# SyncE's order of the stacking and maxima transfers, and the place of 24 aggregations, in a patch-attention-feedforward kernel

## The chip, the cores and the metric

The kernel runs on one core of a Trainium2 chip. A core has five engines that run their own instruction streams side by side and wait for each other through semaphores: TensorE (PE), VectorE (DVE), ScalarE (ACT), GpSimd (POOL) and SyncE (SP), which here only issues transfers. The metric is the device time of one execution in microseconds (us), the median of several runs.

## The reference

Sixteen images of 3x64x64 are cut into patches at three scales along a Hilbert curve, embedded, interpolated to 256 tokens of width 192, and fused. Then follow a causal attention with 12 heads of width 16 and a fast feedforward layer, a walk down a binary tree of 21 nodes. Cut to what matters here:

```python
h = tok(x)                                            # (16, 256, 192), 16 images
qkv = (layernorm(h) @ W_attn + b_attn).reshape(16, 256, 3, 12, 16)
scores = einsum("bqhd,bkhd->bhqk", q, k) / 4          # causal mask: -inf above the diagonal
h = h + (softmax(scores) @ v).reshape(16, 256, 192) @ W_proj + b_proj
logits = layernorm(h) @ weights_in.T                  # (16, 256, 21)
# 10 steps: idx = 2 * idx + 1 + (logit[idx] > 0), gelu(logit) as coefficient of each node
h = h + coeff @ weights_out
```

Everything is float32 at the outside.

## The kernel before

**The work.** The images (`b`, 0 to 15) go through a pipeline of steps. In step b the scores of image b are computed for its row maxima, while the transposed scores of image b-1 go through the exponential, are cut to the causal triangle and weighted with the values, and while queries and keys of image b+2 are computed. The softmax needs the maximum of each row ahead of the exponential of the transposed scores, so scores are computed twice: once as rows (`scores`, L1437 and L1441) for VectorE's `row_max` (L933), and once transposed (`scores_t`, L1475 and L1479) for ScalarE's `exp` (L616). The negative maximum enters the transposed product as two more rows of the contraction.

**Parts.** Queries and keys are split into three bfloat16 parts (`PART`): ScalarE writes the first (`first_part`, L604, semaphore `p0_ok`, two calls per image, 3 activations), VectorE the remainder (`rest`, L946), ScalarE the second (`middle`, L610, `p1_ok`), GpSimd the third (`low`, L378, `p2_ok`). Six products of parts are stacked along the contraction: 6 blocks of 16 rows. `stack(f, w, n)` (L320) issues on SyncE the transfers that copy part n of the queries (w = 0, tile `QS` or `QSL`) or keys (w = 1, `KS` or `KSL`) of image f to their blocks: 3 transfers for part 0, 2 for part 1, 1 for part 2, so 12 per image, each 96 KB, from SBUF to SBUF. It waits first until the part is there for both calls. `maxima(b)` (L326) waits for `mt_ok` and issues the 12 KB transfer that puts the maxima of image b, as ScalarE leaves them in `MT` (L621), into rows 96 and 97 of image b's query stack. `scores_t(b, par, 0)` waits for it (`m_in`), `scores(b, par, 0)` for all stacks of image b (`stacked`).

**What sets the order.** Every engine's order is written by hand. SyncE runs its transfers strictly in the order of the code, and an unmet wait holds all behind it. In iteration n of its loop it issues the stacks of image n+1 and then the maxima of image n, so the stacks of image n+2 go behind the maxima of image n. In ScalarE's step b (f = b+2, d = b-1) stand: three exponentials of d, values of f, first part of f (one activation), four exponentials, first part of f (two activations), two exponentials, `middle(f, 0)`, `front`, `maxima(b)` (writes `MT`), `middle(f, 1)`. In TensorE's step b: `scores(b, 0)`, queries, `scores(b, 1)`, values, `scores_t(d, 0)`, `thirds`, and then `scores` and `scores_t` in turn. The stacks have a ring of four buffers, `PART` one of two.

**The first step.** `first_step` on each engine takes the row maxima of image 0 beside the rest of the token work. VectorE aggregates there the statistics of the 24 tiles of images 4 to 15 (`aggregate(OTHERS)`, L898), ScalarE takes the root (`deviations(3, OTHERS)`, L572), VectorE the reciprocal (`rstd(3, OTHERS)`, L906); the first user is the scaling of image 4 on ScalarE in step 1.

Of the kernel before, what the change touches and what calls it, by code (L numbers as in the profile page):

```python
# [5 lines left out]
B, CH, IMG = 16, 3, 64  # L6
# [23 lines left out]
SU = 9  # L30
# [35 lines left out]
def vit_tower_kernel(nc, x0, x1, x2, ix0, ix1, ix2, w0, w1t, w2t, wft, wfn, bcol, bf, bfc,  # L66
# [8 lines left out]
    with ctx:  # L75
# [3 lines left out]
        def sem(name):  # L79
            return ctx.enter_context(nc.semaphore(name))  # L80
# [113 lines left out]
        ht_ps, ht_ok = sem("ht_ps"), sem("ht_ok")  # L194
# [19 lines left out]
        st_ps, exp_ok, av_ps, ot_ok, cut_ok, carried = [sem(n) for n in ("st_ps", "exp_ok", "av_ps", "ot_ok", "cut_ok", "carried")]  # L214
# [29 lines left out]
        HEADS, SECOND, OTHERS = slice(0, 2 * TT), slice(2 * TT, 4 * TT), slice(4 * TT, NT)  # L244

        def parts(b):

            return PART[PARTS * (b.off % 2):PARTS * (b.off % 2 + 1)]
# [31 lines left out]
        def _(sp):  # L280
# [22 lines left out]
            def ones(i):  # L303

                sp.dma_start(KS[i][KQ:KM, :, :].rearrange("r h s -> r (h s)"), onesk).then_inc(ld_ones, 16)
# [9 lines left out]
            def stack(f, w, n):  # L315

                sp.wait_ge((p0_ok, p1_ok, p2_ok)[n], f.count(2, 2))
                dst = (QS, KS)[w][f.off % RING]
                for k in TERMS[w][n]:
                    sp.dma_start(dst[HS * k:HS * (k + 1), :, :].rearrange("r h s -> r (h s)"),  # L320
                                 parts(f)[n][EMB * w:EMB * (w + 1), :, :].rearrange("p m s -> p (m s)")).then_inc(stacked[w][f.off % 2], 16)

            def maxima(b):

                sp.wait_ge(mt_ok, b.count(1, 1))
                sp.dma_start(QS[b.off % RING][KQ:KM, :, :], MT[:, :]).then_inc(m_in, 16)  # L326

            first = Image(0, 0)
            for part in range(PARTS):
                for w in range(2):  # L330
                    stack(first, w, part)
            for n in range(B):
                b, f = Image(0, n), Image(0, n + 1)
                if n + 1 < B:
                    if n == 1:
                        sp.wait_ge(ht_ok, B)
                        ones(2)
                        ones(3)
                    if n > 2:
                        sp.wait_ge(st_ps, SU * (n - 2))  # L340
                    stack(f, 1, 0)
                    stack(f, 0, 2)
                    stack(f, 0, 1)
                    stack(f, 1, 2)
                    stack(f, 0, 0)
                    stack(f, 1, 1)
                maxima(b)

            for k in range(NQ - 1):
                sp.wait_ge(*added(k))  # L350
# [150 lines left out]
        def _(act):  # L501
# [68 lines left out]
            def deviations(round_, tiles):  # L570
                act.wait_ge(var_ok, round_)
                nc.scalar.activation(SD[:, tiles], VE[:, tiles], ACT.Sqrt).then_inc(sd_ok, 1)  # L572
# [45 lines left out]
            def maxima(b):  # L618

                act.wait_ge(mt_ps, b.count(1, 1))  # L620
                nc.scalar.mul(MT[:, :], BANK[O_BANK[1]][0:2 * H, 0:S // 2].bitcast(bf16), -1.0).then_inc(mt_ok, 1)  # L621
# [66 lines left out]
            first, second = Image(0, 0), Image(0, 1)  # L688

            def first_step():  # L690

                tokens(1, 5)
                front(Image(0, 2))
                tokens(1, 6)
                norm(Image(0, 3))
                tokens(1, 7)
                values(Image(0, 2))
                first_part(Image(0, 2), 0)
                first_part(Image(0, 2), 1)
                deviations(3, OTHERS)  # L700
                middle(Image(0, 2), 0)
                middle(Image(0, 2), 1)
                front(Image(0, 3))
                maxima(first)

            patches_t(0, 0)
            patches_t(0, 1)
# [110 lines left out]
        def _(dve):  # L818
# [76 lines left out]
            def aggregate(tiles):  # L895
                dve.wait_ge(stat, done[0])
                for k in range(tiles.start, tiles.stop):
                    nc.vector.bn_aggr(MV[:, k, :], ST[:, k, :]).then_inc(stat, 1)  # L898
                    done[0] += 1
                dve.wait_ge(stat, done[0])  # L900
                variances(tiles)

            def rstd(round_, tiles):

                dve.wait_ge(sd_ok, round_)
                nc.vector.reciprocal(RSTD[:, tiles], SD[:, tiles]).then_inc(rstd_ok, 1)  # L906
# [136 lines left out]
            first, second = Image(0, 0), Image(0, 1)  # L1043

            def first_step():

                row_max(first, 0, 0)
                row_max(first, 0, 1)
                row_max(first, 0, 2)
                statistics(1, 4)  # L1050
                row_max(first, 0, 3)
                statistics(1, 5)
                row_max(first, 0, 4)
                statistics(1, 6)
                row_max(first, 0, 5)
                statistics(1, 7)
                row_max(first, 0, 6)
                rest(Image(0, 2), 0)
                rest(Image(0, 2), 1)
                aggregate(OTHERS)  # L1060
                row_max(first, 0, 7)
                row_max(first, 0, 8)
                rstd(3, OTHERS)

            def first_low():
# [817 lines left out]
```

## Time and profile before

| | us |
|---|---|
| median of 3 runs | 324.56 |
| the three runs | 324.44, 324.56, 325.06 |
| the profiled execution | 324.9 |
| its span, first to last instruction | 323.2 |
| TensorE busy | 268.2 (83%) |
| VectorE busy | 240.4 (74%) |
| ScalarE busy | 202.4 (63%) |
| GpSimd busy | 196.5 (61%) |
| mean granted clock of TensorE | 0.966 of full |

Busy time is what an engine's instructions took; SyncE's issues of transfers are not counted as busy. The transfers of SyncE's queue take 33.7% of the 16 DMA engines' span. The span is that of the profiled execution, and all durations and places of the trace are from it, in us from its start. The time from issue to landing of a stacking transfer is 2.9 us at least, 3.6 in the median and 5.4 at most.

### The profile page before, as it was taken

How to read it: one execution, taken by the hardware profiler on the slowest of the kernel's cores; microseconds unless marked ns; L12 is line 12 of the kernel's file. 1: busy time of each engine (PE TensorE's matmuls, PEld its weight loads, DVE VectorE, ACT ScalarE, POOL GpSimd, SP SyncE). 2: the span in 40 equal slices, each digit the busy share in tenths (PEclk: the TensorE clock that was granted, in tenths of full speed). 3: DMA queues.
4: the chain of work that ended last, by engine and by line, in shares of the span. 5: the costliest groups of instructions: out<-in, count | busy, mean ns of one | idle time of the engine just before them, and what ended most of it. 6: DMA issues, size and time to landing. Idle time of an engine off the chain costs nothing.

```text
span 323.2 us, 7904 instructions
## 1 busy us (share of the span) xinstructions
PE 268.2 (83%) x2506; PEld 196.8 (61%) x2506; DVE 240.4 (74%) x1156; ACT 202.4 (63%) x429; POOL 196.5 (61%) x419
## 2 busy tenths in 40 slices
PE   0499887188787789999999999999989989999872
PEld 0465655077765466666666666667657578777662
DVE  2053887147496839999999999999989988876872
ACT  2653293047346918868778877876865854868770
POOL 3737777500204827778687778688668666556561
PEclk9999999679999959999999999999999999999997
DMA  5822332003970942444434534524432333000039
GB/s 126 235 54 39 85 69 44 16 2 77 130 89 31 125 119 30 114 84 102 125 85 101 129 87 99 127 90 100 110 102 88 110 103 52 2 4 3 0 107 285
DMA packets 27456, 28.13 MB, mean 87 GB/s; under 512 B 7186, under 2 KB 26704, under 8 KB 27416
## 3 DMA queue, kind: packets, MB, share of 16 engines
q1 hardware_dynamic: 23912, 24.56, 33.7%
q0 software_dynamic: 1568, 2.36, 3.2%
q10 hardware_dynamic: 1936, 0.72, 0.9%
q8 instruction: 20, 0.33, 0.5%
q14 instruction: 20, 0.16, 0.2%
HBM read 4.62 MB, written 3.15 MB: 24 GB/s over the span
## 4 chain that ended last, share of the span: by engine, by line
PE 41%; DVE 20%; POOL 14%; issue 9%; DMA 6%; SPq 5%; ACT 4%; POOLq 0%; ACTq 0%; DVEq 0%
POOL G L373 9%; DVE C L933 9%; PE bank L1497 6%; PE bank L1441 5%; SPq L320 4%; PE bank L1475 4%; PE bank L1412 3%; PE bank L1437 2%; PE bank L1500 2%; DMA G<-x,I 2%; POOL PT L400 2%; PE bank L1382 2%; PE bank L1530 2%; ACT PT L616 2%; PE bank L1479 2%
## 5 line engine op out<-in xcount | busy, mean ns | idle before, releaser
L933 DVE CUSTOM_DVE_ANT_0 C<-bank,MASKV 128x256 bf16<-128x256 f32 (+1 forms) x384 | 111.8, 352 | 18.8 <-PE bank L1441 11.2
L616 ACT ACTIVATE PT<-bank 128x512 f32<-128x512 f32 x144 | 81.8, 602 | 40.2 <-PE bank L1475 32.1
L400 POOL TENSOR_SCALAR_AFFINE_SELECT PT<-PT 128x256 f32<-128x256 f32 x144 | 66.4, 473 | 0.0
L396 POOL TENSOR_TENSOR CARRY<-CARRY 1x1 f32<-1x1 f32 x96 | 17.6, 183 | 46.7 <-ACT PT L616 46.7
L378 POOL TENSOR_TENSOR PART<-RES,PART 128x256 bf16<-128x256 f32 (+1 forms) x31 | 28.0, 904 | 21.1 <-ACT PART L610 21.1
L373 POOL DMA_INDIRECT G<-x,I x32 | 30.3, 947 | 14.2 <-issue 9.4
L1497 PE MATMUL bank<-PT,VA 128*32 128x256 f32 x384 | 30.7, 390 | 4.6 <-POOL PT L400 4.6
L933 DVE DVE_READ_ACCUMULATOR2_ANT MX<- 128x1 f32 x384 | 32.2, 84 | 0.0
L946 DVE SCALAR_TENSOR_TENSOR RES<-bank,BQK,PART 128x256 f32<-128x256 f32 x48 | 21.5, 478 | 1.1 <-ACT PART L604 1.1
L604 ACT ACTIVATE PART<-bank,BQK 128x256 bf16<-128x256 f32 x48 | 21.0, 481 | 1.8 <-PE bank L1397 1.8
L1441 PE MATMUL bank<-KS,QS 96*128 96x256 bf16 x96 | 18.6, 275 | 2.0 <-DVE MX L933 1.8
L1475 PE MATMUL bank<-QS,KS 98*128 98x256 bf16 x96 | 19.0, 279 | 0.6 <-DMA QS<-MT 0.6
L1500 PE MATMUL bank<-PT,VA 128*32 128x128 f32 x384 | 19.4, 273 | 0.0
L1441 PE MATMUL bank<-KSL,QSL 96*128 96x256 bf16 x96 | 18.9, 279 | 0.5
L1475 PE MATMUL bank<-QSL,KSL 98*128 98x256 bf16 x96 | 18.2, 273 | 0.0
L1382 PE MATMUL bank<-SCT,RW 128*128 128x256 f32 x64 | 18.1, 407 | 0.0
L610 ACT CAST PART<-RES 128x256 bf16<-128x256 f32 (+1 forms) x32 | 16.1, 507 | 2.4 <-DVE RES L946 1.3
L1500 PEld LDWEIGHTS bank<-PT,VA 128*32 128x32 f32 x384 | 12.7, 110 | 8.0
L889 DVE BATCH_NORM_STATS2 ST<-HT 128x6 f32<-128x192 f32 x32 | 9.5, 348 | 10.7 <-ACT HT L567 10.6
L1423 PE MATMUL bank<-WP 128*128 128x192 f32 x82 | 15.7, 331 | 1.3 <-DVE HT L1187 1.3
L1497 PEld LDWEIGHTS bank<-PT,VA 128*32 128x32 f32 x384 | 7.9, 108 | 13.6 <-POOL PT L400 9.8
L1360 PE MATMUL bank<-RH,LH 128*128 128x192 f32 x64 | 14.0, 362 | 2.5 <-ACT HT L567 1.3
(181 smaller groups left out, 625.1 us busy)
## 6 DMA issues: line engine op xcount, KB each, us to landing
QS<-PART SPq DMA_DIRECT2D x48, 96.0 KB, 3.6
KS<-PART SPq DMA_DIRECT2D x48, 96.0 KB, 3.6
KSL<-PART SPq DMA_DIRECT2D x48, 96.0 KB, 3.4
QSL<-PART SPq DMA_DIRECT2D x48, 96.0 KB, 3.7
out<-HT SPq DMA_DIRECT2D x7, 384.0 KB, 3.6
G<-x,I POOLq DMA_INDIRECT x42, 4.7
RW<-ZW SPq DMA_DIRECT2D x16, 36.0 KB
WA<-wa SPq DMA_DIRECT2D x1, 432.0 KB, 4.0
```

What stands on the lines that cost most here:

```text
L373: pool.indirect_dma_start(G0[:, t, F0 * g:F0 * (g + 1), :].rearrange("p f b -> p (f b)"), None, x0, bass.IndirectOffsetOnAxis(ap=I0[:, j:j ...
L378: pool.tensor_tensor(parts(b)[2][:, ROUNDS[w], :], RES[:, ROUNDS[w], :], parts(b)[1][:, ROUNDS[w], :], ALU.subtract).then_inc(p2_ok, 1)
L400: pool.affine_select(out=e, in_=e, compare_op=ALU.is_ge, fill=0.0, base=0, pattern=[[0, n], [1, P]], channel_multiplier=-1).then_inc(cut_o ...
L604: ins = nc.scalar.activation(parts(b)[0][:, m, :], bank[:, n * S:(n + 1) * S], ACT.Identity, bias=BQK[:, m:m + 1])
L616: nc.scalar.activation(PT[:, v, :], BANK[T_BANK[(SU * par + v) % 2]][:, :], ACT.Exp, scale=SCALE).then_inc(exp_ok, 1)
L933: ins = nc.vector.tensor_tensor_reduce(JUNK[:, n:n + keys], bank[:, j * keys:(j + 1) * keys], MASKV[:, S - keys:S], 1.0, LOWEST, ALU.add, ...
L946: ins = nc.vector.scalar_tensor_tensor(RES[:, m, :], bank[:, n * S:(n + 1) * S], BQK[:, m:m + 1], parts(b)[0][:, m, :], ALU.add, ALU.subtract)
L1382: ins = nc.tensor.matmul(BANK[MB][:, m * S:(m + 1) * S], RW[:, b.off, m * P:(m + 1) * P], SCT[:, :], start=m == 0, stop=m == 1)
L1441: ins = nc.tensor.matmul(bank[:, j * S:(j + 1) * S], QS[b.off % RING][0:KQ, h, P:S], KS[b.off % RING][0:KQ, h, :], start=j == 0, stop=j == 1)
L1475: ins = nc.tensor.matmul(bank[:, j * S:(j + 1) * S], KS[b.off % RING][:, h, 0:P], QS[b.off % RING][:, h, :], start=j == 0, stop=j == 1)
L1497: nc.tensor.matmul(bank[32 * j:32 * j + 32, c:c + S], VA[b.off % VRING][:, 0, 4 * g + j, :], PT[:, 3 * g + j // 2, (j % 2) * S:(j % 2 + 1) ...
L1500: ins = nc.tensor.matmul(bank[32 * j:32 * j + 32, c + P:c + S], VA[b.off % VRING][:, 1, 4 * g + j, :], PT[:, 3 * g + 2, j * P:(j + 1) * P] ...
```

## The change

SyncE's loop runs one image further ahead. The stacks of image 1 go all ahead, in the order part 0, part 1, part 2; the ones rows for the ring's last two buffers follow them, and the stacks of image 2 lie around the maxima of image 0: first and second parts ahead, third parts behind. From iteration 1 on, the first parts of image n+2 (3 transfers of keys, 3 of queries) go ahead of the maxima of image n, and its second and third parts (6 transfers) behind. The diff counts parts from 0: `stack(f, w, 0)` is a first part. On VectorE `aggregate(OTHERS)` goes behind the last two row maxima of image 0, and on ScalarE `deviations(3, OTHERS)` behind `maxima(first)`.

```diff
--- before.py
+++ after.py
@@ -329,22 +329,36 @@
             for part in range(PARTS):
                 for w in range(2):
                     stack(first, w, part)
-            for n in range(B):
-                b, f = Image(0, n), Image(0, n + 1)
-                if n + 1 < B:
-                    if n == 1:
-                        sp.wait_ge(ht_ok, B)
-                        ones(2)
-                        ones(3)
-                    if n > 2:
-                        sp.wait_ge(st_ps, SU * (n - 2))
+            second, third = Image(0, 1), Image(0, 2)
+            stack(second, 1, 0)
+            stack(second, 0, 0)
+            stack(second, 0, 1)
+            stack(second, 1, 1)
+            stack(second, 0, 2)
+            stack(second, 1, 2)
+            sp.wait_ge(ht_ok, B)
+            ones(2)
+            ones(3)
+            stack(third, 1, 0)
+            stack(third, 0, 0)
+            stack(third, 0, 1)
+            stack(third, 1, 1)
+            maxima(first)
+            stack(third, 0, 2)
+            stack(third, 1, 2)
+            for n in range(1, B):
+                b, f = Image(0, n), Image(0, n + 2)
+                if n + 2 < B:
+                    if n > 1:
+                        sp.wait_ge(st_ps, SU * (n - 1))
                     stack(f, 1, 0)
+                    stack(f, 0, 0)
+                maxima(b)
+                if n + 2 < B:
+                    stack(f, 0, 1)
+                    stack(f, 1, 1)
                     stack(f, 0, 2)
-                    stack(f, 0, 1)
                     stack(f, 1, 2)
-                    stack(f, 0, 0)
-                    stack(f, 1, 1)
-                maxima(b)
 
             for k in range(NQ - 1):
                 sp.wait_ge(*added(k))
@@ -697,11 +711,11 @@
                 values(Image(0, 2))
                 first_part(Image(0, 2), 0)
                 first_part(Image(0, 2), 1)
-                deviations(3, OTHERS)
                 middle(Image(0, 2), 0)
                 middle(Image(0, 2), 1)
                 front(Image(0, 3))
                 maxima(first)
+                deviations(3, OTHERS)
 
             patches_t(0, 0)
             patches_t(0, 1)
@@ -1057,9 +1071,9 @@
                 row_max(first, 0, 6)
                 rest(Image(0, 2), 0)
                 rest(Image(0, 2), 1)
-                aggregate(OTHERS)
                 row_max(first, 0, 7)
                 row_max(first, 0, 8)
+                aggregate(OTHERS)
                 rstd(3, OTHERS)
 
             def first_low():
```

The order on SyncE in the steady part, eleven rows around one maxima transfer. `KSL` and `QSL` are key and query stacks, `MT` the maxima; the names in brackets are the semaphores waited for. The line numbers are those of each kernel. Before, the stretch from the stacks of image 5 to the maxima of image 4:

```order
81 L320 DMA KS<-PART 16x4x768 [waits p0_ok,st_ps]
82 L320 DMA KS<-PART 16x4x768 x2
83 L320 DMA QS<-PART 16x4x768 [waits p2_ok]
84 L320 DMA QS<-PART 16x4x768 [waits p1_ok]
85 L320 DMA QS<-PART 16x4x768
86 L320 DMA KS<-PART 16x4x768 [waits p2_ok]
87 L320 DMA QS<-PART 16x4x768 [waits p0_ok]
88 L320 DMA QS<-PART 16x4x768 x2
89 L320 DMA KS<-PART 16x4x768 [waits p1_ok]
90 L320 DMA KS<-PART 16x4x768
91 L326 DMA QS<-MT 2x12x256 [waits mt_ok]
```

Now, the first parts of image 5, the maxima of image 3 behind them, and the rest of image 5:

```order
80 L320 DMA KS<-PART 16x4x768 [waits p0_ok,st_ps]
81 L320 DMA KS<-PART 16x4x768 x2
82 L320 DMA QS<-PART 16x4x768 [waits p0_ok]
83 L320 DMA QS<-PART 16x4x768 x2
84 L326 DMA QSL<-MT 2x12x256 [waits mt_ok]
85 L320 DMA QS<-PART 16x4x768 [waits p1_ok]
86 L320 DMA QS<-PART 16x4x768
87 L320 DMA KS<-PART 16x4x768 [waits p1_ok]
88 L320 DMA KS<-PART 16x4x768
89 L320 DMA QS<-PART 16x4x768 [waits p2_ok]
90 L320 DMA KS<-PART 16x4x768 [waits p2_ok]
```

The six transfers that wait for `p0_ok` now stand together, and the maxima's transfer directly behind them; before it stood behind a whole image of stacks whose parts had been finished a step ago.

The same on SyncE at the start, from the stacks of image 2 to a maxima transfer. Before, with the maxima of image 1 at the end:

```order
48 L320 DMA KSL<-PART 16x4x768 [waits p0_ok]
49 L320 DMA KSL<-PART 16x4x768 x2
50 L320 DMA QSL<-PART 16x4x768 [waits p2_ok]
51 L320 DMA QSL<-PART 16x4x768 [waits p1_ok]
52 L320 DMA QSL<-PART 16x4x768
53 L320 DMA KSL<-PART 16x4x768 [waits p2_ok]
54 L320 DMA QSL<-PART 16x4x768 [waits p0_ok]
55 L320 DMA QSL<-PART 16x4x768 x2
56 L320 DMA KSL<-PART 16x4x768 [waits p1_ok]
57 L320 DMA KSL<-PART 16x4x768
58 L326 DMA QS<-MT 2x12x256 [waits mt_ok]
```

Now, with the maxima of image 0 in their midst:

```order
47 L320 DMA KSL<-PART 16x4x768 [waits p0_ok]
48 L320 DMA KSL<-PART 16x4x768 x2
49 L320 DMA QSL<-PART 16x4x768 [waits p0_ok]
50 L320 DMA QSL<-PART 16x4x768 x2
51 L320 DMA QSL<-PART 16x4x768 [waits p1_ok]
52 L320 DMA QSL<-PART 16x4x768
53 L320 DMA KSL<-PART 16x4x768 [waits p1_ok]
54 L320 DMA KSL<-PART 16x4x768
55 L326 DMA QS<-MT 2x12x256 [waits mt_ok]
56 L320 DMA QSL<-PART 16x4x768 [waits p2_ok]
57 L320 DMA KSL<-PART 16x4x768 [waits p2_ok]
```

Before, the maxima of image 0 stood ahead of all of these; now ten of the twelve transfers of image 2 stand ahead of them.

On VectorE in the first step, before (`ISA C,MX` is a row maximum, L946 the remainder of image 2):

```order
150 L946 SCALAR_TENSOR_TENSOR RES<-bank,BQK,PART 128x256 [waits p2_ok,p0_ok] x2
151 L946 SCALAR_TENSOR_TENSOR RES<-bank,BQK,PART 128x256
152 L898 BN_AGGR MV<-ST 128x2 [waits stat]
153 L898 BN_AGGR MV<-ST 128x2 x23
154 L893 TENSOR_SCALAR VE<-MV 128x24 [waits stat]
155 L933 ISA C,MX<-bank,MASKV 128x256 [waits s_ps]
156 L933 ISA MX 128x1
```

Now, the place on VectorE where the aggregations stood:

```order
150 L960 SCALAR_TENSOR_TENSOR RES<-bank,BQK,PART 128x256 [waits p2_ok,p0_ok] x2
151 L960 SCALAR_TENSOR_TENSOR RES<-bank,BQK,PART 128x256
152 L947 ISA C,MX<-bank,MASKV 128x256 [waits s_ps]
153 L947 ISA MX 128x1
154 L947 ISA C,MX<-bank,MASKV 128x256
```

And the place on VectorE to which they went, behind the last row maximum of image 0:

```order
158 L947 ISA C,MX<-bank,MASKV 128x256
159 L947 ISA MX 128x1
160 L912 BN_AGGR MV<-ST 128x2 [waits stat]
161 L912 BN_AGGR MV<-ST 128x2 x23
162 L907 TENSOR_SCALAR VE<-MV 128x24 [waits stat]
```

The 24 aggregations and the addition to the variances stand behind the eight instructions of the last two row-maximum groups; in the changed kernel the line numbers from here on are 14 higher.

## Rows read from the trace of the kernel before

**Rows 1.** Page, part 1: busy time, share of span, instructions
```profile
PE 268.2 (83%) x2506; PEld 196.8 (61%) x2506; DVE 240.4 (74%) x1156; ACT 202.4 (63%) x429; POOL 196.5 (61%) x419
```

**Rows 2.** Timeline of SyncE, 100 to 112: start, duration, line, transfer, count
```profile
100.71 0.71 SPq L326 DMA_DIRECT2D QS<-MT  x1
...
102.62 1.87 SPq L320 DMA_DIRECT2D KSL<-PART  x3
104.54 1.87 SPq L320 DMA_DIRECT2D QSL<-PART  x3
106.45 0.59 SPq L320 DMA_DIRECT2D KSL<-PART  x1
...
109.00 1.24 SPq L320 DMA_DIRECT2D KSL<-PART  x2
```

**Rows 3.** Chain that ended last, 92 to 130: start, duration, what
```profile
109.64 4.78 DMA KSL<-PART
```

**Rows 4.** Timeline of SyncE, 222 to 235
```profile
222.48 0.65 SPq L326 DMA_DIRECT2D QSL<-MT  x1
...
234.21 0.65 SPq L326 DMA_DIRECT2D QSL<-MT  x1
```

**Rows 5.** Timeline of TensorE in four stretches: start, duration, line, count, [idle before, releaser]
```profile
99.99 0.28 PE L1456 MATMUL bank<-IDB,MP 128*24 128x128 bf16 x2 [1.08 <-POOL MP L410]
...
102.96 0.39 PE L1475 MATMUL bank<-QS,KS 98*128 98x256 bf16 x2 [0.56 <-DMA QS<-MT]
...
114.66 0.59 PE L1437 MATMUL bank<-KSL,QSL 96*128 96x128 bf16 x4 [2.25 <-DMA KSL<-PART]
...
118.56 0.63 PE L1475 MATMUL bank<-QS,KS 98*128 98x256 bf16 x2
...
225.22 0.38 PE L1475 MATMUL bank<-QSL,KSL 98*128 98x256 bf16 x2
...
261.61 0.38 PE L1475 MATMUL bank<-QS,KS 98*128 98x256 bf16 x2
```

**Rows 6.** Windows: stretch, its length, busy time by engine, granted clock, DMA share
```profile
109.95:112.41 2.46, 1.15 (x20) 0.52 (x18) 1.37 (x3) 1.69 (x6) 2.37 (x7) 1.00 1.06 121
112.41:114.66 2.25, 0.00 (x1) 0.03 (x2) 0.75 (x2) 0.66 (x3) 2.00 (x4) 0.78 0.45 107
114.66:120.50 5.84, 5.84 (x22) 4.45 (x23) 2.20 (x13) 0.60 (x1) 0.77 (x1) 0.50 0.45 118
234.90:235.95 1.05, 0.08 (x5) 0.05 (x2) 0.88 (x3) 1.04 (x4) 0.80 (x2) 1.00 0.04 12
```

**Rows 7.** Timeline of ScalarE in two stretches
```profile
92.92 1.20 ACT L604 ACTIVATE PART<-bank,BQK 128x256 bf16<-128x256 f32 x3 [0.18 <-PE bank L1397]
...
103.39 1.74 ACT L616 ACTIVATE PT<-bank 128x512 f32<-128x512 f32 x3 [0.36 <-PE bank L1475]
...
107.82 0.84 ACT L604 ACTIVATE PART<-bank,BQK 128x256 bf16<-128x256 f32 x2
...
225.64 1.74 ACT L616 ACTIVATE PT<-bank 128x512 f32<-128x512 f32 x3 [1.43 <-PE bank L1475]
...
230.25 0.83 ACT L604 ACTIVATE PART<-bank,BQK 128x256 bf16<-128x256 f32 x2
...
233.81 0.37 ACT L621 ACTIVATE MT<-bank 24x256 bf16<-24x256 bf16 x1 [0.45 <-PE bank L1456]
```

**Rows 8.** SyncE's L320, window 102.5 to 103.0: first transfer of a string
```profile
L320 SPq DMA_DIRECT2D KSL<-PART x1: 606/606/606, 102.6 to 102.6; - x1
...
DMA to landing us min/median/max: 3.0/3.0/3.0
```

**Rows 9.** The same, window 105.8 to 106.2: the sixth
```profile
L320 SPq DMA_DIRECT2D QSL<-PART x1: 594/594/594, 105.8 to 105.8; - x1
...
DMA to landing us min/median/max: 3.9/3.9/3.9
```

**Rows 10.** The same, window 79.3 to 79.4: a seventh
```profile
L320 SPq DMA_DIRECT2D QS<-PART x1: 592/592/592, 79.3 to 79.3; - x1
...
DMA to landing us min/median/max: 3.8/3.8/3.8
```

**Rows 11.** Timeline of VectorE around the aggregations
```profile
96.08 1.68 DVE L898 BATCH_NORM_AGGREGATE MV<-ST 128x2 f32<-128x6 f32 x24
```

## The prediction

> **What bounds the kernel now.** I read the busy shares first, then SyncE's own rows, since the change mostly reorders SyncE, then the chain, and then the rows of TensorE and ScalarE around what SyncE feeds. TensorE is busy 83% and VectorE 74% of a span of 323.2 us [rows 1]. A step (one image's scores and row maxima beside the previous image's exponentials) takes about 11.7 us: SyncE's issue of the maxima stands at 222.48 and again at 234.21, 11.73 later [rows 4]. Over the long stretch, the first transposed-score matmul (L1475) of image 1 starts at 118.56 and that of image 13 at 261.61 [rows 5]: 143.05 us for 12 steps, 11.92 each. The reader is to see two things more. First, one large stall: SyncE issues the twelve stacking transfers of image 2 in one string from 102.62 to 110.2, one per 0.64 us (102.62 to 106.45 is six, 3.83 us) [rows 2]; the last lands 4.78 us after its issue, at 114.4 [rows 3], and TensorE has stood 2.25 us at it [rows 5]. Its clock falls meanwhile (0.78 granted on average in 112.41 to 114.66, then 0.50, the 1.2 GHz level, until 120.50) [rows 6]. Second, the transfer of the maxima goes at once when ScalarE has MT: MT ends at 233.81 + 0.37 = 234.18 and the issue starts at 234.21 [rows 7, 4]. Everything ahead of it on SyncE was issued before.
>
> **The change, part 1: the six transfers ahead of the maxima.** In step n SyncE now has to issue K and Q first parts of image n+2 (six transfers) and only then the maxima of image n. The six wait for both first parts of image n+2, which ScalarE ends at 230.25 + 0.83 = 231.08 [rows 7]. Six issues take 3.83 us [rows 2], so the maxima go at 234.95 and not at 234.21: 0.74 late. That alone would be covered, for the consumer starts 225.22 - 222.48 = 2.74 us after the issue in a full-speed step [rows 4, 5], and the transfer needs at most 102.96 - 100.71 = 2.25 us with an empty queue, where TensorE waited for it [rows 2, 5].
>
> But the queue is no longer empty. No row shows the maxima issued 0.64 us behind six stacking transfers. The nearest rows: in the string from 102.62 the first landed 3.0 us after its issue and the sixth (105.82) 3.9 us after, at 109.7 [rows 8, 9]. A maxima transfer issued next, at 106.45, and landing behind it, needs 3.3 us. Bounds: 2.25 us if it passes them, and 3.8 us if it behaves like the seventh large one in a row, which was issued at 79.31 [rows 10]. I take 3.3, near the upper rows, since twelve in a row visibly queue (4.78) and nothing in the rows shows a transfer overtaking.
> The page "DMA: Bandwidth & Descriptors" of the Trainium skill (section "Queues, rings and completion order") says that the increment of a semaphore lands only after all earlier writes of the same DMA engine, which keeps the 3.3 and the sum below. Its section "Why a DMA increments its semaphore by 16 and not by 1" says that a transfer uses only as many engines as divide its outermost sizes: the maxima, with 2 rows, would use two, and would wait for the backlog of those two alone; by that rule the landing lies between the bounds, and in their middle (2.8) the time would be about 328 us. No row here separates the two.
>
> **What this closes.** The delay is not paid once. The maxima of image n-1 release its transposed scores, these its exponentials, and between them in ScalarE's order stand the first parts of image n+2, which SyncE now needs before the maxima of image n. One round, from the landing of one maxima to the next:
> - L1475 start to first exponential on ScalarE: 225.64 - 225.22 = 0.42 [rows 5, 7].
> - ScalarE, seven exponentials, the values and three first parts without a gap: in the step where TensorE held it least 103.39 to 107.82 + 0.84 = 108.66, 5.27 us [rows 7]; in a common step 225.64 to 231.08, 5.44. I take 5.27.
> - six issues 3.83, and 0.05 to the next issue.
> - landing 3.3 (2.25 to 3.8).
> Sum 12.87 us (11.82 to 13.37, and 13.54 with the 5.44), against 11.92 now. The round holds for the maxima of images 1 to 13, that is 12 rounds: 154.4 us. In it TensorE stands about 1.4 us at L1475 in every step, with VectorE behind it, because the next row maxima need scores that stand behind L1475 on TensorE.
>
> **Part 2: the second parts behind the maxima.** Behind the maxima only these six go, and for the last of them 6 issues and a landing of 3.9 us are 7.7 us after the maxima's issue, where a step has 11.7 or more: they are in well before TensorE wants them. That takes away the stall of 2.2 us, and the few lesser ones of the same kind: 143.05 less 12 times the undisturbed 11.73 is 2.3 us in all for what is lost at full clock and in the rest of the slow one. These savings are inside the comparison of 154.4 with 143.05 and are not subtracted again.
>
> **Part 3: the start.** The first parts of image 2 are ready at 92.92 + 1.20 = 94.12 [rows 7]. Six issues end at 97.95, four more (its second parts, ready by then) at 100.51. So the first maxima go at 100.55, where they go at 100.71 now [rows 2]. They stand behind ten transfers: I take 3.5 us to land (2.25 to 4.5), at 104.05, against 102.96 now. One round of 12.87 later, at 116.9, image 1's would be in. In between TensorE stands with nothing to do. Now its work ahead of that matmul ends at 102.96 - 0.56 = 102.40 and starts with the maxima's transpose at 99.99, behind an idle 1.08 us [rows 5]; with the row maxima earlier (part 4) both move up by about 1 us. So it stands from about 101.4 to 104.05, longer than the 2.25 us in which its clock fell. A fall costs what it costs now: TensorE was busy for all 5.84 us at 0.50, so about half of that, 2.9 us [rows 6]. Since the stretch ahead is fuller than it was there (1.15 of 2.46 us busy [rows 6]), I put half of the 2.9 into the sum: 118.3 for image 1's transposed scores, where they start at 118.56 now. The start gives 0.3 us.
>
> **Part 4: the 24 aggregations.** They take 1.68 us [rows 11] ahead of the last two row maxima and go behind them, so MT of image 0 is ready up to 1.7 us earlier. SyncE reaches it only at 100.55 (above), so nothing comes of it. What moves behind is covered: VectorE has from about 97.6 and ScalarE from about 99.7 until 104.05. ScalarE fits the scaling of image 4 between its issue of MT and 103.39 now, with 0.36 us to spare [rows 7], and has 0.7 us more then, for a square root and for VectorE's reciprocal ahead of it. If the first maxima landed at 102.8 instead, that margin would be about gone and up to 0.5 us would show, once.
>
> **The sum.** Image 13's transposed scores start at 118.3 + 154.4 = 272.7, where they start at 261.61 now: 11.1 us later. Behind that TensorE's order is unchanged and nearly without gaps, so I carry the 11.1 through. The profiled execution took 324.9 us for a span of 323.2; 336.0 for the same kind of run, and the median of three runs before, 324.56, is 0.34 below the profiled one: **335.7 us**.
>
> **Rivals.**
> (A) The maxima pass the stacking transfers (landing 2.25). For: it has 12 KB where the others have 96, and ahead of it the string has only six, not twelve. Against: a landing that grows from 3.0 to 4.78 along a string. Then the maxima of image 0 are in at 102.8, a round is 11.82 us, image 1's at 114.6, and image 13's at 114.6 + 141.8 = 256.4, 5.2 us earlier than now: 319 us. This is the other side. The point from which it decides is a landing of about 2.6 us: 12 rounds of 12.17 from 115.3 end at 261.3. Each 0.1 us of landing is worth 1.3 us of time.
> (B) TensorE's clock falls in every step, at the new wait of 1.4 us. For: it fell in the 2.2 us. Against: it kept 1.00 over 234.90 to 235.95, where TensorE was busy for 0.08 of 1.05 us [rows 6]. Price: up to 2.9 us in each of 12 steps, 35 us: about 370 us.
> (C) The late maxima cost just what the stall gave, within 0.2% (0.65 us). It takes a landing within 0.05 us of the 2.6 above: 325 us.
>
> **How the numbers follow.** The forecast, with landings from above 2.6 to 3.8: 0.80; A: 0.12; B: 0.05; C: 0.03. What a measurement of this kernel can tell from no change is 0.2%. So slower 0.85, same 0.03, faster 0.12. The range: 325 (landing 2.6) to 342 (landing 3.6, 12 rounds of 13.17 = 158.0, behind a start at 120.2 with the whole price of the clock: 16.6 us). It leaves out A, B and landings above that, about 2 in 10.
>
> **What would show it.** In the profile after: six stacking transfers of SyncE directly ahead of the maxima's in each step, and the maxima's 0.04 us behind them, not behind MT; a wait of TensorE "L1475 <- DMA QS<-MT" in most steps, of 1 to 1.5 us; steps of 12.5 to 13.2 us; no wait of L1437 for a stacking transfer; the aggregations not in the chain. Wrong would be: steps of 11.7 to 11.9 with the L1475 wait absent or under 0.3 us (then A), or a granted clock of 0.5 in a part of every step (then B).

## The result, and the profile after

The changed kernel takes **338.15 us** (median of 4 runs, 337.83 to 342.14), where the kernel before takes 324.74 beside it (324.44 to 325.06). The ratio is 1.0441, with a 95% interval of 1.0363 to 1.052: slower. The profiled run took 338.23 us for a span of 336.5, against 324.9 and 323.2. Predicted were 335.7 us in a range of 325 to 342. Part of the runs of every kernel here, the one before included, take 4 to 5 us longer than its shortest; in those of them that were profiled, the last of the first gathers lands at 68 us of the span and not at 63. Line numbers behind the diff are 14 higher than before (L1475 is now L1489, L616 is L630, L1441 is L1455).

The page of the kernel after, busy time by engine, and the chain that ended last by engine ("issue" is time in which an engine waited for nothing that the profile shows):

```profile
PE 271.0 (81%) x2506; PEld 197.7 (59%) x2506; DVE 241.7 (72%) x1156; ACT 202.2 (60%) x429; POOL 196.1 (58%) x419
...
PE 28%; SPq 18%; DMA 18%; ACT 15%; POOL 9%; issue 8%; DVE 4%; ACTq 0%; DVEq 0%; POOLq 0%
```

The same chain by engine before:

```profile
PE 41%; DVE 20%; POOL 14%; issue 9%; DMA 6%; SPq 5%; ACT 4%; POOLq 0%; ACTq 0%; DVEq 0%
```

The engines do the work of before [rows 1]; TensorE alone has 2.8 us more, and no run takes that apart. The chain has changed its kind. Before, SyncE's issues (SPq) made up 5% of it and transfers 6%; now they make up 18% each, and ScalarE 15%. That is what a ring through a queue looks like: no engine is fuller, and all wait.

The chain of the kernel after through one round, 176 to 196: start, duration, what.

```profile
179.02 3.28 DMA QSL<-MT
...
182.44 0.38 PE bank L1489 x2
...
187.40 0.74 ACT PART L618 x2
...
188.20 0.55 SPq L320
...
191.97 3.32 DMA QSL<-MT
...
195.43 0.38 PE bank L1489 x2
```

The reader is to see that it closes on itself: maxima land, L1489 runs, ScalarE comes to the first parts (L618), SyncE issues six transfers, then the maxima, and they land 3.32 us later. SyncE's rows of the same stretch (the columns as in [rows 4]):

```profile
182.86 7.16 SPq L320 DMA_DIRECT2D KS<-PART  x4
190.06 1.87 SPq L320 DMA_DIRECT2D QS<-PART  x3
191.97 0.65 SPq L326 DMA_DIRECT2D QSL<-MT  x1
```

ScalarE's:

```profile
182.85 1.74 ACT L630 ACTIVATE PT<-bank 128x512 f32<-128x512 f32 x3 [2.82 <-PE bank L1489]
...
187.29 0.83 ACT L618 ACTIVATE PART<-bank,BQK 128x256 bf16<-128x256 f32 x2
```

The four K rows are one transfer of a third part and the three of the next first part, which had to wait for ScalarE until 188.12. The round is then 182.85 - 182.44 = 0.41, ScalarE 5.27 (to 187.29 + 0.83), 0.08, six issues 3.77 (188.20 to 191.97), landing 3.32, and 0.14 to the matmul: 12.99. The landing is not the same in every round: of the thirteen behind six stacking transfers (images 1 to 13) eleven took 3.24 to 3.46 us, the one of image 2 took 2.68, and the one of image 9 took 2.52; the mean is 3.23. For image 9 SyncE needed 4.30 us and not 3.77 for its six issues, so the bytes ahead had longer to land:

```profile
218.61 2.52 DMA QS<-MT
```

TensorE shows the price of the ring:

```profile
104.12 0.39 PE L1489 MATMUL bank<-QS,KS 98*128 98x256 bf16 x2 [2.41 <-DMA QS<-MT]
...
117.94 0.38 PE L1489 MATMUL bank<-QS,KS 98*128 98x256 bf16 x2 [1.30 <-DMA QS<-MT]
...
182.44 0.38 PE L1489 MATMUL bank<-QSL,KSL 98*128 98x256 bf16 x2 [1.26 <-DMA QSL<-MT]
...
273.23 0.39 PE L1489 MATMUL bank<-QS,KS 98*128 98x256 bf16 x2 [1.82 <-DMA QS<-MT]
```

Waits of the kernel after: waited for, us in total, times, longest.

```profile
DVE C L947 <- PE bank L1455: 25.3, 29, 3.9
...
PE bank L1489 <- DMA QS<-MT: 12.2, 8, 2.4
...
PE bank L1489 <- DMA QSL<-MT: 7.1, 6, 1.3
```

TensorE waits for the maxima 14 times, 19.3 us in all. VectorE, whose row maxima need scores that stand behind L1489, waits with it. From image 1 to image 13, L1489 goes from 117.94 to 273.23: 155.29 us, 12.94 a round, where [rows 5] have 143.05. Image 13 is 11.62 us late. The span is 13.3 longer, so 1.68 us are lost behind image 13. The windows show a slow clock there (stretch, length, busy PE, PEld, DVE, ACT, POOL, granted clock, DMA share, GB/s):

```profile
182.44:195.43 12.99, 11.24 (x118) 7.63 (x119) 11.18 (x61) 9.02 (x21) 9.01 (x22) 1.00 0.36 93
104.45:107.86 3.41, 3.41 (x20) 2.51 (x19) 1.58 (x11) 2.42 (x6) 1.40 (x5) 0.50 0.00 0
...
273.30:275.10 1.80, 1.80 (x21) 1.74 (x22) 0.15 (x1) 1.06 (x2) 0.00 (x0) 1.00 0.70 136
275.10:278.50 3.40, 3.40 (x23) 2.90 (x21) 2.38 (x17) 2.50 (x5) 1.64 (x5) 0.50 0.17 35
```

The clock falls to the 1.2 GHz level for 3.4 us at the start, where before it was there for longer [rows 6], and once more at 275.1, behind the wait of 1.82 us for image 13. It does not fall in the rounds between (1.00 over the whole of the one shown).

### The profile page after: what moved, and what is told of

Its sections match the earlier page's. It is cut to its first block, busy times and chain, and to the rows that moved or that the text cites. A ratio compares the mean times of both kernels' runs of the same rounds, so it can differ in the third digit from the quotient of the medians.

```text
span 336.5 us, 7904 instructions
## 1 busy us (share of the span) xinstructions
PE 271.0 (81%) x2506; PEld 197.7 (59%) x2506; DVE 241.7 (72%) x1156; ACT 202.2 (60%) x429; POOL 196.1 (58%) x419
## 3 DMA queue, kind: packets, MB, share of 16 engines
HBM read 4.62 MB, written 3.15 MB: 23 GB/s over the span
## 4 chain that ended last, share of the span: by engine, by line
PE 28%; SPq 18%; DMA 18%; ACT 15%; POOL 9%; issue 8%; DVE 4%; ACTq 0%; DVEq 0%; POOLq 0%
SPq L320 17%; POOL G L387 9%; DMA QS<-MT 8%; ACT PT L630 7%; DMA QSL<-MT 6%; ACT PART L618 5%; PE bank L1489 5%; DMA G<-x,I 2%; PE bank L1493 2%; PE bank L1411 2%; PE bank L1544 2%; ACT VA L608 2%; PE bank L1374 2%; PE bank L1451 1%; DMA KS<-PART 1%
## 5 line engine op out<-in xcount | busy, mean ns | idle before, releaser
L630 ACT ACTIVATE PT<-bank 128x512 f32<-128x512 f32 x144 | 81.4, 602 | 53.3 <-PE bank L1489 44.9
L410 POOL TENSOR_TENSOR CARRY<-CARRY 1x1 f32<-1x1 f32 x96 | 17.6, 183 | 61.5 <-ACT PT L630 61.5
L1489 PE MATMUL bank<-QS,KS 98*128 98x256 bf16 x96 | 19.6, 287 | 12.3 <-DMA QS<-MT 12.2
L1489 PE MATMUL bank<-QSL,KSL 98*128 98x256 bf16 x96 | 18.2, 274 | 7.2 <-DMA QSL<-MT 7.1
L618 ACT ACTIVATE PART<-bank,BQK 128x256 bf16<-128x256 f32 x48 | 20.9, 480 | 1.8 <-PE bank L1411 1.8
L1455 PE MATMUL bank<-KS,QS 96*128 96x256 bf16 x96 | 19.1, 281 | 1.8 <-DVE MX L947 1.8
L1455 PE MATMUL bank<-KSL,QSL 96*128 96x256 bf16 x96 | 18.8, 278 | 0.1
L1489 PEld LDWEIGHTS bank<-QS,KS 98*128 98x128 bf16 x96 | 8.2, 103 | 17.7 <-issue 9.9
L1514 PEld LDWEIGHTS bank<-PT,VA 128*32 128x32 f32 x384 | 12.7, 110 | 8.0
L1396 PE MATMUL bank<-SCT,RW 128*128 128x256 f32 x64 | 17.2, 390 | 0.0
L1437 PE MATMUL bank<-WP 128*128 128x192 f32 x82 | 15.7, 331 | 1.3 <-DVE HT L1201 1.3
```

The lines of the kernel that those rows point to most:

```text
L618: ins = nc.scalar.activation(parts(b)[0][:, m, :], bank[:, n * S:(n + 1) * S], ACT.Identity, bias=BQK[:, m:m + 1])
L630: nc.scalar.activation(PT[:, v, :], BANK[T_BANK[(SU * par + v) % 2]][:, :], ACT.Exp, scale=SCALE).then_inc(exp_ok, 1)
L1455: ins = nc.tensor.matmul(bank[:, j * S:(j + 1) * S], QS[b.off % RING][0:KQ, h, P:S], KS[b.off % RING][0:KQ, h, :], start=j == 0, stop=j == 1)
L1489: ins = nc.tensor.matmul(bank[:, j * S:(j + 1) * S], KS[b.off % RING][:, h, 0:P], QS[b.off % RING][:, h, :], start=j == 0, stop=j == 1)
L1514: ins = nc.tensor.matmul(bank[32 * j:32 * j + 32, c + P:c + S], VA[b.off % VRING][:, 1, 4 * g + j, :], PT[:, 3 * g + 2, j * P:(j + 1) * P] ...
```

## The experiments

**The theory**: the round of 12.9 us is a ring through SyncE, and two of its terms are the change's own, the six issues and a landing that the six make late. **The rivals**: the landing is late whatever stands ahead; or the issues alone close the ring; or the start carries the loss. Each ratio is to the kernel before, run beside. Profiled runs are compared by the length of their steps, or from the first step's L1455 row with "[0.97 <-DVE MX" on (95.51 in the kernel after; 95.04 before, where the line is L1441; the line numbers of the other runs differ from after's by up to three).

**1. No stacks of the image after next ahead of the maxima.**

```diff
             for n in range(1, B):
+                maxima(b)
                 if n + 2 < B:
...
                     stack(f, 0, 0)
-                maxima(b)
-                if n + 2 < B:
                     stack(f, 0, 1)
```

> The changed kernel with the maxima of image n ahead of all stacking transfers of image n+2 from iteration 1 on; its start and its order of parts are kept. Theory (a closed round: six issues and a landing behind their backlog stand in every step between one maxima transfer and the next): the round is gone, steps fall back to 11.7 us, TensorE has no wait at L1489 for the maxima, and 12 steps of 11.73 from about 116.6 (where TensorE comes to image 1's transposed scores in the changed kernel) give 257.4 where the kernel before has 261.6: about 320.5 us (319 to 322). Rival R1 (the loss comes from the earlier stacking traffic as such, which disturbs the engines): 330 us or more. Rival R2 (the loss comes from the start and the second parts' order): stays near 338.

Measured: 324.99 us in the median (320.07 to 326.07, 11 runs), ratio 0.9876 (0.981 to 0.9942). Four runs took 320.07 to 321.04. Most steps take 11.73, and the twelve from image 1 to 13 take 139.99, where the kernel after has 155.29. L1489 (here L1488) waits for a maxima transfer once, in the first step:

```profile
PE bank L1488 <- DMA QS<-MT: 2.7, 1, 2.7
```

The whole loss is in the place of the steady maxima. The changed start, which this kernel keeps, loses nothing: on the scale of before (4.67 us less) image 1's transposed scores start at 117.57, for 118.56.

**2. Only the three key transfers ahead.**

```diff
                     stack(f, 1, 0)
-                    stack(f, 0, 0)
                 maxima(b)
                 if n + 2 < B:
+                    stack(f, 0, 0)
                     stack(f, 0, 1)
```

> The changed kernel with only the three key transfers of the first part ahead of the maxima; the three query transfers behind. Theory: three issues end 1.9 us after the first parts are ready, while MT is ready 3.1 us after them, so the issue isn't late, and the third transfer lands before a quiet maxima transfer would: same as none ahead, about 320.5 us (319 to 323), steps of 11.7. Rival (every transfer ahead costs its share): about half of the loss, 329 us, steps of 12.3.

Measured: 325.06 in the median (319.86 to 325.76, 10 runs), ratio 0.9975 (0.9909 to 1.0041), which alone decides nothing; two runs took 319.86 (the profiled one) and 320.32. SyncE in it:

```profile
169.19 1.82 SPq L320 DMA_DIRECT2D KS<-PART  x3
172.24 0.65 SPq L326 DMA_DIRECT2D QSL<-MT  x1
```

and TensorE:

```profile
174.96 0.39 PE L1489 MATMUL bank<-QSL,KSL 98*128 98x256 bf16 x2
```

The issues of the key transfers end at 171.01, and SyncE waits 1.2 us for MT, as before. L1489 starts 2.72 us after the issue and waits for nothing. Steps are 11.73: with three ahead the ring is open. So it is not whether stacks stand ahead, but how much of them.

**3. Five ahead** (the sixth behind the maxima).

```diff
                     stack(f, 1, 0)
-                    stack(f, 0, 0)
+                    stack(f, 0, 0, slice(0, 2))
                 maxima(b)
                 if n + 2 < B:
+                    stack(f, 0, 0, slice(2, 3))
```

> The changed kernel with five of the six first-part transfers ahead of the maxima and one query transfer behind, from iteration 1 on. Theory: five issues end 3.2 us after the first parts, where MT is ready after 3.1, so the issue is late by 0.1 only, but the landing is that behind five (3.0 to 3.2): round 0.42 + 5.27 + 3.19 + 0.05 + 3.1 + 0.14 = 12.2 us, 12 steps 146: about 328.5 us (327 to 330). Rival (only an issue later than MT costs): round 11.8, 322 us.

Measured: 330.44 in the median (326.77 to 332.9, 12 runs), ratio 1.0083 (1.0023 to 1.0143); five runs took 326.77 to 327.17. SyncE:

```profile
178.97 0.65 SPq L326 DMA_DIRECT2D QSL<-MT  x1
...
191.09 0.65 SPq L326 DMA_DIRECT2D QSL<-MT  x1
```

and TensorE:

```profile
182.19 0.38 PE L1490 MATMUL bank<-QSL,KSL 98*128 98x256 bf16 x2 [0.42 <-DMA QSL<-MT]
```

The round shown takes 12.12, and the twelve from image 1 to 13 take 145.82, 12.15 each. By the ring's terms it is 0.41 + 5.27 + 0.08 + five issues 3.15 + 3.22 (issue to L1490) = 12.13. The last term is read from this run (a landing of 3.08, for 3.28 behind six), so this shows that the terms add up; the forecast made from them ahead of the run was 12.2. One transfer less takes 0.8 us off each round, and the wait at this matmul goes from 1.26 to 0.42.

**4. The six first parts small** (from image 4 on 8 KB where they have 96; the stacks hold old data there, and the scores of these images are not the reference's).

```diff
                 for k in TERMS[w][n]:
+                    if n == 0 and f.off >= 4:
+                        sp.dma_start(dst[HS * k:HS * (k + 1), 0, :], parts(f)[n][EMB * w:EMB * w + HS, 0, :]).then_inc(stacked[w][f.off % 2], 16)
+                        continue
```

> The changed kernel with the same six issues ahead of the maxima, but from image 4 on each of the six copies 16 rows of 512 bytes (8 KB) and not 96 KB, so most of the first parts are left out of the stacks. Theory (landing behind the backlog is a part of the round): issues stay at 0.64 us each, the landing of the maxima falls from 3.3 to about 2.25, rounds from 13.0 to 11.9 or 12.0 us in 11 steps: 326 to 327 us. Rival (only the lateness of the issue costs, the landing is 3.3 whatever the backlog): 338 us, rounds of 13.0.

Measured: 326.85 in the median (323.03 to 329.78, 10 runs), ratio 0.9996 (0.9944 to 1.0047). From image 2's L1492 to image 13's the rounds are 11.68 to 11.82, with one of 12.09. SyncE:

```profile
178.64 1.85 SPq L321 DMA_DIRECT2D QS<-PART  x3
180.53 0.67 SPq L329 DMA_DIRECT2D QSL<-MT  x1
```

and TensorE:

```profile
182.77 0.38 PE L1492 MATMUL bank<-QSL,KSL 98*128 98x256 bf16 x2
```

and the landing in a round where TensorE waited for it (from the chain):

```profile
216.17 2.16 DMA QS<-MT
```

This separates the two terms. The six issues take as long as ever (0.62 us apiece), and the maxima stand directly behind them; but L1492 starts 2.24 us after their issue with no wait for them, where L1489 of the same image starts 3.42 after it in the kernel after. The difference of 1.2 is the whole excess of its round, 12.95 against 11.75. It is the bytes ahead and not the number of instructions that make the landing late. An empty queue gives the same time, 2.25 from issue to matmul [rows 2, 5]. The six issues alone bring the ring to 0.41 + 5.27 + 0.08 + 3.75 + 2.24 = 11.75, just the length that a step has anyway; they cost almost nothing alone, but with them the whole late landing is paid. I had expected rounds of 11.9 to 12.0 and was 0.15 too high.

**5. ScalarE issues the maxima, past SyncE's queue.**

```diff
             def maxima(b):
-                sp.wait_ge(mt_ok, b.count(1, 1))
-                sp.dma_start(QS[b.off % RING][KQ:KM, :, :], MT[:, :]).then_inc(m_in, 16)
...
+                act.wait_ge(mt_ok, b.count(1, 1))
+                act.dma_start(QS[b.off % RING][KQ:KM, :, :], MT[:, :]).then_inc(m_in, 16)
```

> The changed kernel with the transfer of the maxima issued by ScalarE right behind MT, SyncE's order of the stacking transfers kept. Theory: the maxima go when MT is ready and no longer behind six issues; five stacking transfers are still in flight, so they land 2.25 (nothing in common with SyncE's queue) to 3.0 us (behind what the same DMA engines have) after the issue; the round is 11.1 to 11.9 us and the engines' own 11.73 decides: steps of 11.7 to 11.9. The first maxima go at about 100.0 and not at 101.06. 12 steps from about 115.8: 257 to 259 where the kernel before has 261.6: 320 us (318.5 to 322). Rival (a transfer on the other queue lands no sooner than SyncE's sixth): steps of 12.5, 328 us. A price of ScalarE's own issue of 0.6 us per step would be hidden in its wait for TensorE.

Measured: 329.14 in the median (326.17 to 331.29, 4 runs), ratio 1.0136 (0.9948 to 1.0325, unclear), the profiled run 327.32. Steps are 12.2 and not the 11.7 to 11.9 I expected: a miss. The chain of it:

```profile
173.49 0.38 ACT MT L634
173.89 3.27 DMA QSL<-MT
```

The transfer starts 0.02 us behind MT, on another queue, with five of the six stacking transfers issued, and still lands 3.27 us later (3.14 to 3.38 in the rounds of images 1 to 13). ScalarE's queue is not slow by itself. For image 14, with all stacks long in, the matmul comes 2.57 us after the issue and waits for nothing:

```profile
273.43 0.62 ACTq L636 DMA_DIRECT2D QSL<-MT  x1
...
276.00 0.38 PE L1490 MATMUL bank<-QSL,KSL 98*128 98x256 bf16 x2
```

So an own queue does not get it past the stacks in flight. The ring is now another one, without SyncE: maxima, L1490, the rest of the step (TensorE's for the most part), MT, maxima. In [rows 4, 5] the issue is followed by the matmul after 2.74 us in a step of 11.73; here it takes 3.27 + 0.14 = 3.41, and the step is 0.5 longer. I had missed that a landing of 3.3 costs by itself, wherever the issue stands. This agrees with the Trainium skill, page "DMA: Bandwidth & Descriptors", section "Queues, rings and completion order": an increment lands only after the earlier writes of the same DMA engine, across its queues. The run cannot tell that from a plain share of the engines' time.

**6. The aggregations and ScalarE's root back where they were.**

```diff
                 first_part(Image(0, 2), 1)
+                deviations(3, OTHERS)
                 middle(Image(0, 2), 0)
...
+                aggregate(OTHERS)
                 row_max(first, 0, 7)
                 row_max(first, 0, 8)
-                aggregate(OTHERS)
```

> The changed kernel with only the 24 aggregations and the square root back in their old places. Theory: MT of image 0 is ready 1 us later (about 100.7), and the second parts of image 2 come later too, since ScalarE's middle stands behind the root again (ready at about 99.0); SyncE ends its ten issues at about 101.6 and not 101.0, so the first maxima go 0.5 us later and the whole is 0.5 us slower, 338.6 us, ratio to before 1.042 to 1.046. What was written at the forecast, that nothing comes of it, would be 338.1. Rival (the moved aggregations are a part of the loss, by ScalarE's later scaling of image 4): 336 us or less.

Measured: 339.66 in the median (335.87 to 342.27, 6 runs), ratio 1.0365 (1.0287 to 1.0442), the same as the kernel after within what these runs tell. But the place is not idle. The chain of it:

```profile
101.51 1.61 DVE MV L912 x24
...
103.36 0.22 ACT SD L586
103.58 0.82 ACT PART L624 x2
...
107.20 2.69 DMA QS<-MT
```

ScalarE waits for the aggregations ahead of its second parts of image 2, and SyncE waits for these with the maxima behind them. From the L1455 row (here 4.88 later than after's), the first maxima go at 102.32 where they go at 101.06 after, and L1489 starts at 105.05 for 104.12. By image 13 nothing of it is left: 277.79 - 4.88 = 272.91, for 273.23. What took it up is open, since this run also had a full clock at the start and landings of only 2.44 to 3.09 us for images 1 to 4. The clock fell neither at the start nor behind image 13, though TensorE stood 2.19 us at image 0, 1.74 at image 1 and 1.79 at image 13:

```profile
277.79 0.39 PE L1489 MATMUL bank<-QS,KS 98*128 98x256 bf16 x2 [1.79 <-DMA QS<-MT]
```

From there to the end are 339.3 - 277.79 = 61.5 us, for 63.3 after and 61.6 before. That is the loss of 1.68 behind image 13, gone with the fall of the clock.

**7. TensorE kept busy at the two waits** (matmuls into a free bank ahead of L1489 in the first step and at image 13).

```diff
+                    if b.first:
+                        keep_busy(bank, 7)
                     if b.off >= B - 3:
-                        keep_busy(bank, 3)
+                        keep_busy(bank, 8 if b.off == B - 3 else 3)
```

> The changed kernel with idle matmuls put ahead of the two waits behind which the granted clock fell: 7 of 0.33 us ahead of image 0's first transposed scores, 8 and not 3 ahead of image 13's. Nothing else. Theory: both falls (3.4 us at 0.50 each) go away, each is worth up to 1.7 us: 335 us (334 to 336.5). Rival (behind the falls TensorE isn't on the path): 338.

Measured: 336.47 in the median (334.6 to 341.32, 6 runs), ratio 1.0339 (1.0268 to 1.041). Windows and TensorE's rows:

```profile
277.67:281.00 3.33, 3.33 (x37) 3.05 (x38) 1.62 (x13) 2.44 (x5) 0.66 (x3) 1.00 0.56 110
...
122.10:126.10 4.00, 3.97 (x24) 3.21 (x25) 2.08 (x15) 2.92 (x7) 1.63 (x5) 0.57 0.40 98
```

```profile
108.60 0.39 PE L1491 MATMUL bank<-QS,KS 98*128 98x256 bf16 x2 [0.24 <-DMA QS<-MT]
...
122.13 0.38 PE L1491 MATMUL bank<-QS,KS 98*128 98x256 bf16 x2 [1.95 <-DMA QS<-MT]
...
277.67 0.39 PE L1491 MATMUL bank<-QS,KS 98*128 98x256 bf16 x2 [0.19 <-DMA QS<-MT]
```

Behind image 13 the clock stays up, and from L1491 to the end are 339.6 - 277.67 = 61.9 us, for 63.3 after and 61.6 before. That is the lost 1.7, less 0.3; experiment 6 gives all of it. At the start the fall only moves to the next wait, a step later, and little seems gained: on the scale of after (4.38 us less) L1491 of image 1 starts at 117.75 for 117.94. But that is two things that cancel. ScalarE from its first exponential to its last first part, in the kernel after:

```profile
104.55 0.60 ACT L630 ACTIVATE PT<-bank 128x512 f32<-128x512 f32 x1 [1.27 <-PE bank L1489]
...
109.93 0.83 ACT L618 ACTIVATE PART<-bank,BQK 128x256 bf16<-128x256 f32 x2
```

and here, and below it one of SyncE's six issues of this round, from the chain:

```profile
109.03 1.74 ACT L630 ACTIVATE PT<-bank 128x512 f32<-128x512 f32 x3 [1.37 <-PE bank L1491]
...
113.47 0.83 ACT L618 ACTIVATE PART<-bank,BQK 128x256 bf16<-128x256 f32 x2
```

```profile
115.56 1.45 SPq L320
```

Under the slow clock the first exponentials wait for TensorE, and ScalarE's member of the ring takes 6.21 us; at full clock it takes 5.27. So the fall at the start costs 0.94. Here one issue took 1.45 us and not 0.59, SyncE needed 4.64 for the six and not 3.77, and 0.87 of the gain was lost again.

**8. What the runs point to: three ahead in every step, and at the start the first maxima right behind the six first parts.**

```diff
             stack(third, 0, 0)
+            maxima(first)
             stack(third, 0, 1)
             stack(third, 1, 1)
-            maxima(first)
...
                     stack(f, 1, 0)
-                    stack(f, 0, 0)
                 maxima(b)
                 if n + 2 < B:
+                    stack(f, 0, 0)
```

> The changed kernel with three key transfers ahead of the maxima from iteration 1 on (steps of 11.73 were seen in that form), and the first maxima behind the first parts of image 2 alone, ahead of its second parts. Theory: the first maxima go when MT is there, about 100.0, and not at 101.06 behind four more issues; little backlog, landing 2.3 to 2.6, image 0's transposed scores at about 102.6 and not 104.1; TensorE idles about 0.9 us there and not 2.4, so its clock keeps 2.4 GHz. Gain over the form with only the three ahead (319.9): 1.5 and up to 1.7 for the clock: 317 us (316 to 319), 0.975 to 0.98 of before. Rival (the second parts of image 2, now later, are the next to be waited for at step 2, or the start is not on the path): 319.9 as without.

Measured: 319.88 in the median (317.05 to 322.74, 6 runs), ratio 0.9746 (0.9661 to 0.983); three runs took 317.05 to 317.76, the profiled one among them. It beats both kernels. SyncE:

```profile
96.83 1.86 SPq L320 DMA_DIRECT2D QSL<-PART  x3
100.29 0.70 SPq L326 DMA_DIRECT2D QS<-MT  x1
```

and TensorE:

```profile
102.56 0.39 PE L1489 MATMUL bank<-QS,KS 98*128 98x256 bf16 x2 [0.58 <-DMA QS<-MT]
...
114.48 0.38 PE L1489 MATMUL bank<-QS,KS 98*128 98x256 bf16 x2
```

SyncE waits for MT again, the first maxima are used 2.27 us after their issue, TensorE stands 0.58 and keeps its clock, and the stall of 2.25 us at the stacks of image 2 [rows 5] is gone. Image 1's transposed scores start at 114.48 (113.74 on the scale of before) and not at 118.56, and steps are 11.73. So taking stacks ahead is worth something in both places. At the start image 1 gains 1.0 us in experiment 1, 2.4 in experiment 2 and 4.8 here, with the first maxima early; and the twelve steps behind it take 139.9 to 140.0 us in all three, for 143.05 before. Six ahead of the steady maxima buried it.

## Why the prediction held

- **The ring** was right in its place and its members. Predicted 12.87 a round, measured 12.94. Issues 3.83 (3.77), ScalarE 5.27 (5.27), landing 3.3 (3.23 in the mean, 2.52 to 3.46); what was missing are the 0.14 from landing to matmul. Experiments 1 to 4 vary issues and bytes: none or three ahead open the ring, five take off one transfer, and small ones bring it down to the length that a step has anyway. ScalarE's 5.27 was not varied; it is read from the chain.
- **The landing of 3.3** was chosen between 2.25 and 3.8 with no row for it, worked out from stacking transfers of eight times the size; that it fits so well is luck in part. Experiments 3 and 4 stand beside it: 3.08 behind five full transfers, 2.16 behind six small ones. Rival A (2.25, 319 us) falls, and so does the middle value of 2.8.
- **The start** was put at 118.3 for image 1, and came at 117.94. Its parts were less right. The maxima went at 101.06, not 100.55: ScalarE's first parts ended 0.5 us later, as did the L1455 row in this run. The clock's fall was half as long as I took it (3.4 us), and it costs 0.94 (experiment 7), where half of 2.9 stood in the sum.
- **Part 4** has the right sum, nothing that is left by image 13, but a failed step. Part 3 calls the second parts "ready by then", and part 4 gives the aggregations no share in that; experiment 6 shows that it is so only because these were moved. With them back, the first maxima go 1.26 us later (0.28 of it is one long issue).
- **"I carry the 11.1 through"** is the step that missed. Behind image 13 another 1.68 us went, in a second fall of the clock that I had not looked for. The balance of the profiled run, 338.23 for a forecast of 336.0: the start -0.36, the 12 rounds +0.89, the clock +1.68, which is 2.21 of the 2.23.
- **Part 2** was right in its main point: no wait of L1451 (L1437 before) for a stack behind the first step. It counts the stall of 2.2 us among what the twelve steps save, but that stall ended at 114.66, ahead of the first of them [rows 5]; the 2.3 us were lost elsewhere, no run says at what, and the sum doesn't change.
- **The other rivals.** B (a fall in every step) did not happen: the clock was 1.00 over the whole of a steady round. C needs a landing of 2.6 in every round; behind six full transfers two rounds of the thirteen come near it, and the mean is 3.23.
- **The range.** By its own terms its upper end is 324.56 + 16.6 = 341.2 and not 342; the result lies inside either.

## What to carry to other kernels

A small transfer on which an engine's next step hangs lands later for the bytes issued just ahead of it (here by 1.1 us for six of 96 KB); another queue did not free it, fewer bytes ahead did. Before moving transfers ahead of it, follow their own wait back: if what they wait for is itself released by the small transfer, the delay closes to a ring and is paid in every step, and its length is simply the sum of its members. Up to the slack (here three transfers of six) it costs nothing, so count how many fit.

## What was not expected of the hardware

- A 12 KB transfer lands 2.16 us after its issue behind six of 8 KB and 3.24 to 3.46 behind six of 96 KB in most rounds, and 3.14 to 3.38 when another engine issues it to another queue while these are in flight. The issue takes SyncE the same 0.62 to 0.64 us for 8 as for 96 KB.
- Single issues of SyncE took 0.8 to 2.2 us and not 0.59, in every kernel profiled, at places that differ from one to the next (1.45 at 115.56 in experiment 7). No run shows why. Where SyncE was held up among the six, the landing behind them was shorter (2.52 for image 9).
- The clock does not go by the length of one stand alone. It stayed at 2.4 GHz through stands of 1.3 us in nearly every round of the kernel after, and through 2.19, 1.79 and 1.74 in experiment 6. It fell behind 2.41 and 1.82 in the kernel after, and behind 1.95 in experiment 7. What decides stays open.
